# Sparse attention and expert layer on one core: late keys of diagonal tiles zeroed on GpSimd instead of pushed out on TensorE

## What is computed

```python
q, k, v = (sparsify(proj(w), 1) for w in (wq, wk, wv))    # 16 heads of 16; only the largest feature of each is kept
scores = einsum('bhqd,bhkd->bhqk', q, k) / 4
scores = where(key_index > query_index, -inf, scores)      # causal
keep the 64 largest scores of each query, softmax over them
out = einsum('bhqk,bhkd->bhqd', attn, v); out = out @ wo.T
x = x + ga * out                                           # then norm, router, experts
```

## Time and profile before

| | us |
|---|---|
| runs: median (lowest to highest) | 1067.7 (1066.64 to 1073.47) |
| span of the profiled execution, first to last instruction | 1065.8 |
| TensorE, busy in the span | 914.5 |
| VectorE | 662.4 |
| ScalarE | 480.1 |
| GpSimd | 268.7 |

### The profile page before, as it was taken

One profiled execution on the slowest core, in us unless ns is written; L12 is line 12 of the kernel. 1 busy time (PEld: TensorE's weight loads), 2 busy tenths in 40 slices (PEclk: granted clock), 3 DMA queues, 4 the chain that ended last, 5 costly groups with the idle time before them and its releaser, 6 DMA issues. The chain is left out here.

```text
span 1065.8 us, 17246 instructions
## 1 busy us (share of the span) xinstructions
PE 914.5 (86%) x6504; PEld 497.0 (47%) x6504; DVE 662.4 (62%) x1469; ACT 480.1 (45%) x631; POOL 268.7 (25%) x403
## 2 busy tenths in 40 slices
PE   6778999898999988999998999997204999999996
PEld 5533343444444443544445445335102666666664
DVE  6758677568587676676874775735487555543441
ACT  2635767664567745466773654661000122221110
POOL 3603222411331312122230220001003433343322
PEclk9869999999999998999998998998555999999999
DMA  4000000000100002100002011101561244442211
GB/s 145 15 1 21 1 21 1 1 1 2 61 21 1 1 2 81 60 1 2 1 1 81 2 41 44 38 1 40 198 221 37 51 114 107 112 115 41 25 20 20
DMA packets 34854, 46.57 MB, mean 44 GB/s; under 512 B 2184, under 2 KB 30928, under 8 KB 34640
## 3 DMA queue, kind: packets, MB, share of 16 engines
q1 hardware_dynamic: 28624, 36.89, 10.4%
q0 software_dynamic: 6144, 8.52, 5.0%
HBM read 32.69 MB, written 12.72 MB: 43 GB/s over the span
## 5 line engine op out<-in xcount | busy, mean ns | idle before, releaser
L947 ACT ACTIVATE p_buf<-ps 128x1024 f32<-128x1024 f32 x288 | 279.4, 1023 | 181.3 <-PE ps L424 95.6
L424 PE MATMUL ps<-qx,kd 32*128 32x512 f32 (+3 forms) x1280 | 147.0, 536 | 29.8 <-DVE p_buf L1281 26.1
L457 PE MATMUL ps<-p_buf,vv 128*17 128x512 f32 (+3 forms) x1664 | 156.1, 477 | 0.0
L2108 ACT ACTIVATE h_t<-ps,b_t 128x512 f32<-128x512 f32 x64 | 44.0, 688 | 236.7 <-PE ps L2048 236.7
L1281 DVE SCALAR_TENSOR_TENSOR p_buf<-ps,p_buf 128x1024 f32<-128x1024 f32 x64 | 76.7, 1220 | 78.0 <-ACT p_buf L947 65.0
L2048 PE MATMUL ps<-tok_t,w_sb 128*128 128x512 f32 x256 | 113.5, 602 | 0.0
L2058 PE MATMUL ps<-w_sb,h_t 128*128 128x256 f32 x512 | 112.5, 380 | 0.8 <-ACT h_t L2108 0.8
L779 POOL TENSOR_SCALAR_AFFINE_SELECT p_buf<-p_buf 128x512 f32<-128x512 f32 x64 | 42.0, 669 | 272.5 <-ACT p_buf L947 269.7
L2058 PEld LDWEIGHTS ps<-w_sb,h_t 128*128 128x128 f32 x512 | 96.6, 190 | 15.3 <-ACT h_t L2108 1.6
L424 PEld LDWEIGHTS ps<-qx,kd 32*128 32x128 f32 x1280 | 55.2, 191 | 71.6 <-issue 56.2
L365 PE MATMUL ps<-w_t,h_t 128*128 128x512 f32 (+1 forms) x224 | 78.8, 496 | 0.6 <-ACT w_t L889 0.6
(11 more groups left out here) (297 smaller groups left out, 1391.8 us busy)
## 6 DMA issues: line engine op xcount, KB each, us to landing
w_sb<-in_L_ffn_w_dram SPq DMA_DIRECT2D x16, 1024.0 KB, 8.8
h_table<-xr SPq DMA_DIRECT2D x3, 1056.0 KB, 4.6
x_in<-in_L_attn_x_dram SPq DMA_DIRECT2D x6, 512.0 KB, 3.9
out_dram<-xr SPq DMA_DIRECT2D x3, 1024.0 KB, 5.2
xr<-in_L_attn_x_dram SPq DMA_DIRECT2D x3, 1024.0 KB, 5.8
h_table<-xr SPq DMA_DIRECT2D x2, 528.0 KB, 3.0
xr<-in_L_attn_x_dram SPq DMA_DIRECT2D x2, 512.0 KB, 5.3
p_buf<-in_L_wmod_dram SPq DMA_DIRECT2D x1, 1024.0 KB, 8.6
```

Source lines behind the costliest of these rows:

```text
L424: m = pe.matmul(o, key, qx[r, par, t0:t0 + w], start=True, stop=not early)
L457: m = pe.matmul(ps[32 * h:32 * h + HD + 1, 6, o:o + w], vv[:, (gi // NG) % 2, i, HG * (gi % NG) + h, :], p_of(gi, u)[:, h, lo:lo + w], sta ...
L947: act.activation(p_of(gi, u)[:, 2 * a:2 * a + 2, :], buf(w), ACT.Exp, scale=0.25).then_inc(free_of(w)[0], 1)
L2108: act.activation(h1_t[:, f, :], ps[:, L1_BANKS[f % 3], :], ACT.Relu, bias=b1_t[:, e * FO + f:e * FO + f + 1]).then_inc(s_h1, 1)
```

## The change

The running maximum covers the first 256 queries instead of 512 (`RUN`), with the factor 0.625 in place of 0.992; the pieces beyond have no second matmul any more, and the piece of unit 0 with tile 1 has one for its first 128 queries. The matmuls with `late` are gone. GpSimd's `tri` now serves units 0, 1 and 2 too, and all diagonal tiles: eight selects a group instead of four, and `pv` of units 0, 1, 2, 3 and 8 waits for it. The calls `tri(gi, 0)` and `tri(gi, 1)` stand in GpSimd's loop directly ahead of `tri(gi, 2)`. VectorE's scan and product with the queries shrink to 256 columns, and its reduction over the other keys grows from 512 to 768. Left out below: the declaration of `late` and its select at the start, which go.

```diff
--- before.py
+++ after.py
@@ -137,8 +137,9 @@
         q_st = sf("q_st", [P, 2, NT, HG, 2, HD])
         o_tok = sf("o_tok", [P, NT, NH, HD])
 
-        mx = sf("mx", [P, 512])
-        qm = sf("qm", [P, 2, 512], BF16)
+        RUN = 256
+        mx = sf("mx", [P, RUN])
+        qm = sf("qm", [P, 2, RUN], BF16)
         k_far = sf("k_far", [P, T], BF16)
         k_max = sf("k_max", [P, 1])
         k_max1 = sf("k_max1", [P, 1])
@@ -227,7 +227,7 @@
 
         ring_at, m_at, pv_at = {}, {}, {}
 
-        DIAG = (2, 3, 8)
+        DIAG = (0, 1, 2, 3, 8)
 
         def tri_of(gi, u):
             return len(DIAG) * gi + DIAG.index(u) + 1
@@ -412,27 +412,19 @@
                         begin(("S", gi, u, a))
                     lo = 0
                     for i, t0, w in UNITS[u]:
-
-
-                        early = t0 < 512
-                        diag = early and t0 == P * i
+                        run = max(min(RUN - t0, w), 0)
                         last = (i, t0, w) == UNITS[u][-1]
                         for h in range(HG):
                             r = slice(32 * h, 32 * h + 32)
                             o = buf(("S", gi, u, h // 2))[:, h % 2, lo:lo + w]
                             key = ks[r, par, :] if i == 0 else kd[r, par, P * i:P * i + P]
-                            m = pe.matmul(o, key, qx[r, par, t0:t0 + w], start=True, stop=not early)
-                            if h % 2 and last and not early:
+                            m = pe.matmul(o, key, qx[r, par, t0:t0 + w], start=True, stop=not run)
+                            if h % 2 and last and not run:
                                 m.then_inc(full_of(("S", gi, u, h // 2))[0], 1)
-                        for h in range(HG * early):
+                        for h in range(HG * (run > 0)):
                             r = slice(32 * h, 32 * h + 32)
-                            o = buf(("S", gi, u, h // 2))[:, h % 2, lo:lo + w]
-                            m = pe.matmul(o, over[r, :], qm[r, par, t0:t0 + w], start=False, stop=not diag)
-                            if h % 2 and last and not diag:
-                                m.then_inc(full_of(("S", gi, u, h // 2))[0], 1)
-                        for h in range(HG * diag):
-                            o = buf(("S", gi, u, h // 2))[:, h % 2, lo:lo + P]
-                            m = pe.matmul(o, identb[:, :], late[:, :], start=False, stop=True)
+                            o = buf(("S", gi, u, h // 2))[:, h % 2, lo:lo + run]
+                            m = pe.matmul(o, over[r, :], qm[r, par, t0:t0 + run], start=False, stop=True)
                             if h % 2 and last:
                                 m.then_inc(full_of(("S", gi, u, h // 2))[0], 1)
                         lo += w
@@ -460,13 +452,11 @@
 
                 def pv(gi, u):
                     c = 0 if u < 3 else 1
-                    if u in (3, 8):
+                    if u in DIAG:
                         pe.wait_ge(f_tri, tri_of(gi, u))
-                    for a in range(2):
-                        if u in FIRST:
-                            pe.wait_ge(*free_of(("Z", gi, c, a)))
-                        elif u not in (3, 8):
-                            pe.wait_ge(*free_of(("S", gi, u, a)))
+                    else:
+                        for a in range(2):
+                            pe.wait_ge(*free_of(("Z", gi, c, a) if u in FIRST else ("S", gi, u, a)))
                     if gi == 0 and u == 0:
                         pe.wait_ge(f_n0, 1)
                     if u in (0, 3) and 2 * gi + c:
@@ -493,7 +483,6 @@
                         pe.drain().then_inc(f_O, 1)
 
                 def pv_late(gi):
-                    pe.wait_ge(f_tri, tri_of(gi, 2))
                     values(gi, 2, 6, 1, 256, 768, 256).then_inc(f_pv, 1)
                     pv_at[gi, 2] = len(pv_at) + 1
 
@@ -771,10 +760,10 @@
 
                 def tri(gi, u):
                     for a in range(2):
-                        pool.wait_ge(*free_of(("S", gi, u, a)))
+                        pool.wait_ge(*free_of(("Z", gi, 0, a) if u == 1 else ("S", gi, u, a)))
                     lo = 0
                     for i, t0, w in UNITS[u]:
-                        if t0 == P * i and t0 >= 512:
+                        if t0 == P * i:
                             p = p_of(gi, u)[:, :, lo:lo + P]
                             m = pool.affine_select(p, p, [[0, HG], [1, P]], ALU.is_ge, 0.0, base=0, channel_multiplier=-1)
                         lo += w
@@ -807,8 +796,7 @@
                           allow_small_or_imprecise_dtypes=True)
                 pool.iota(tile_no[:, :], [[P, NTALL]], base=0, channel_multiplier=0,
                           allow_small_or_imprecise_dtypes=True)
-                pool.memset(late[:, :], 0.0)
-                pool.memset(over[:, :], -(1.0 - 2.0 ** -7))
+                pool.memset(over[:, :], -0.625)
                 pool.memset(upto[:, :], 1.0)
                 pool.memset(tie[:, :], 0.0)
                 pool.memset(part_r[:, :], 0.0)
@@ -859,6 +846,8 @@
                         first_rstd(b + 1, 0)
                     if tiles:
                         keep(b + 1, t0)
+                    tri(gi, 0)
+                    tri(gi, 1)
                     tri(gi, 2)
                     tri(gi, 3)
                     if g == 0 or g == 3 and pre:
@@ -1118,7 +1107,7 @@
                     dve.tensor_tensor_scan(left[:, h], k_not[:, h], minus1[:, :].to_broadcast([P, 512]), TOPK + 0.5,
                                            ALU.add, ALU.add)
                     dve.drain().then_inc(f_cnr, 1)
-                    dve.tensor_tensor_scan(mx[:, :], kd[:, 0, h], kd[:, 0, h], 0.0, ALU.max, ALU.max)
+                    dve.tensor_tensor_scan(mx[:, :], kd[:, 0, 0:RUN], kd[:, 0, 0:RUN], 0.0, ALU.max, ALU.max)
                     dve.tensor_scalar(k_far[:, h], k_not[:, h], -FAR, None, ALU.mult)
                     dve.scalar_tensor_tensor(kb[:, :], k_not[:, 0:P], FAR, kd[:, 0, 0:P], ALU.mult, ALU.add)
                     dve.scalar_tensor_tensor(k_one[:, :, :], kd[:, 0, 0:P].unsqueeze(1).to_broadcast([P, HG, P]), 0.0,
@@ -1143,15 +1132,15 @@
                     dve.tensor_tensor_scan(left[:, h], k_not[:, h], minus1[:, :].to_broadcast([P, 512]), carry[:, :],
                                            ALU.add, ALU.add)
                     dve.drain()
-                    dve.tensor_reduce(k_max1[:, :], kd[:, 0, h], AX.X, ALU.max)
+                    dve.tensor_reduce(k_max1[:, :], kd[:, 0, RUN:T], AX.X, ALU.max)
                     dve.tensor_scalar(k_far[:, h], k_not[:, h], -FAR, None, ALU.mult)
                     dve.tensor_tensor(n_lo[:, :], n_lo[:, :], left[:, T - 1:T], ALU.min)
                     dve.drain()
-                    dve.tensor_tensor(k_max[:, :], mx[:, 511:512], k_max1[:, :], ALU.max)
+                    dve.tensor_tensor(k_max[:, :], mx[:, RUN - 1:RUN], k_max1[:, :], ALU.max)
                     dve.drain()
                     dve.tensor_scalar(ks[:, 0, :], ks[:, 0, :], k_max[:, :], None, ALU.subtract)
                     dve.scalar_tensor_tensor(kd[:, 0, :], kd[:, 0, :], k_max[:, :], k_far[:, :], ALU.subtract, ALU.add).then_inc(f_kp, 1)
-                    dve.scalar_tensor_tensor(qm[:, 0, :], mx[:, :], k_max[:, :], qx[:, 0, 0:512], ALU.subtract, ALU.mult)
+                    dve.scalar_tensor_tensor(qm[:, 0, :], mx[:, :], k_max[:, :], qx[:, 0, 0:RUN], ALU.subtract, ALU.mult)
 
                 def second_half_queries():
                     dve.wait_ge(f_mfree, m_at["Q1", 0] + 1)
@@ -1229,8 +1218,8 @@
                     par = n % 2
                     kx = kd[:, par, :]
 
-                    dve.tensor_tensor_scan(mx[:, :], kx[:, 0:512], kx[:, 0:512], 0.0, ALU.max, ALU.max)
-                    dve.tensor_reduce(k_max1[:, :], kx[:, 512:T], AX.X, ALU.max)
+                    dve.tensor_tensor_scan(mx[:, :], kx[:, 0:RUN], kx[:, 0:RUN], 0.0, ALU.max, ALU.max)
+                    dve.tensor_reduce(k_max1[:, :], kx[:, RUN:T], AX.X, ALU.max)
                     dve.tensor_scalar(k_far[:, :], k_not[:, :], -FAR, None, ALU.mult)
                     dve.tensor_tensor(n_lo[:, :], n_lo[:, :], left[:, T - 1:T], ALU.min)
                     dve.scalar_tensor_tensor(kb[:, :], k_not[:, 0:P], FAR, kx[:, 0:P], ALU.mult, ALU.add)
@@ -1247,7 +1236,7 @@
                 def queries(n):
                     par = n % 2
                     dve.wait_ge(f_mfree, m_at["Q1", n] + 1)
-                    dve.scalar_tensor_tensor(qm[:, par, :], mx[:, :], k_max[:, :], qx[:, par, 0:512], ALU.subtract, ALU.mult)
+                    dve.scalar_tensor_tensor(qm[:, par, :], mx[:, :], k_max[:, :], qx[:, par, 0:RUN], ALU.subtract, ALU.mult)
                     dve.scalar_tensor_tensor(uq[:, :], qx[:, par, :], 0.0, left[:, :], ALU.is_gt, ALU.mult)
                     dve.tensor_scalar(q_has[:, :], qx[:, par, 0:P], 0.0, 1024.0, ALU.is_gt, ALU.mult)
                     dve.drain().then_inc(f_uq, 1)
```

(2 more changed lines are left out.)

## The result

The changed kernel takes 1095.35 us (median of 4 runs, 1094.17 to 1095.60); the kernel before, beside it, 1070.23. The ratio is 1.0239, with a 95% interval of 1.0205 to 1.0273: slower. The span of the profiled execution went from 1065.8 to 1092.3 us.

A forecast was written before the change was run, and what follows sets the result against it. TensorE's order of work was taken to bound the attention stage. Terms -13.5 + 16.2 + 4.6 + 2.5 - 2.3 + 12.8 = +20.3 us on the 1065.8 span gave 1086.1; adding 1.9 for the median gave 1088, range 1070 to 1104.

The forecast's parts named there:

- Tile groups: Groups 1, 2, 5, 6, 9, 10: selects queue behind keep, TensorE stalls 4.6 us, pv starts 2.7 us later; +16.2 us.
- First groups of a batch: Groups 0, 4, 8: selects queue behind first_rstd; +4.6 us for groups 4 and 8 together, +2.5 for group 0.
- Waits in all: Sign at pv's line: nine waits for GpSimd's select, six about 4.6 us, two about 4.3, one about 8, some 44 us.
- The clock: TensorE after the new stalls: eight new drops to a lower clock at 1.6 us each, +12.8 us.
- Rival (2): TensorE's clock: the stalls come but drops only change their place, giving 1075 us; chance 0.16.
- rival (3): Stalls draw longer clock drops, or VectorE slows the selects in most groups, giving 1104 us; chance 0.10.
- Groups without a stall, and VectorE: Groups 3, 7, 11 to 15 gain 1.93 us each, -13.5; less VectorE work where TensorE waits for its chain, -2.3.
- so the gain stays: In the seven groups without a stall, selects finish while TensorE is still busy, keeping the full 1.93 us per group.
- Rival (1): GpSimd hides all the selects, so only the removed work counts, giving 1034 us; chance 0.06.

The follow-up runs named there:

- order_tiles: Changed kernel with tri(gi, 0) and tri(gi, 1) called ahead of keep but still behind first_rstd on GpSimd; 1054.03 us, ratio 0.9853.
- order_all: Changed kernel with tri(gi, 0) and tri(gi, 1) called ahead of both first_rstd and keep on GpSimd; 1042.05 us, ratio 0.9738.
- fill: Changed kernel with 64 throwaway matmuls of 128 columns ahead of the select wait of unit 0's pv in the nine stalling groups; 1079.97 us, ratio 1.0090.
- max_only: Kernel before the change with only the running maximum cut to 256 queries, late-key matmuls kept; 1058.83 us, ratio 0.9898.
- no_norm: order_all with the eight VectorE instructions of second_norm(b - 1, 0) replaced by four that only signal; 1036.22 us, ratio 0.9680.
- order_norm: order_all plus tri(gi, 2) ahead of first_rstd in groups 0, 4, 8, 12, and VectorE's normalize behind unit 4's two masks; 1026.58 us, ratio 0.9603.

## Why the prediction was right

The direction, the place and nearly the size came out: +20.3 us were worked out on the span, +26.5 came.

- **Tile groups.** Predicted was a stall of 4.6 us with pv 2.7 us late; the six stalls are 4.63 to 4.93, and pv came 2.6 to 3.3 late. With a drop each the six groups were to be 25.8 us longer (16.2 + 6 x 1.6); they are 26.2 longer. Shown by order_tiles and order_all: with the two calls moved, the stalls are gone.
- **First groups of a batch.** Groups 4 and 8: stalls of 4.28 and 4.29 us, as forecast; 8.5 us longer where 7.8 were worked out. Group 0: pv 5.3 us late, as forecast, and 3.1 us net where 2.5 were taken. The wait of unit 5 that was to take up part of it shrank from 3.05 to 0.40.
- **Waits in all.** Some 44 us were forecast for pv's line in nine waits, and 44.0 in nine came; the longest, in group 0, is 7.0 where about 8 was forecast.
- **The clock.** Priced at eight drops of 1.6 us, 12.8; the experiment fill, in which most of them go while the stalls stay, gives 12 to 15. The size came out partly by luck. All nine stalls have a drop, which begins before pv can start and reaches 3.2 to 5.8 us beyond that. In groups 5, 6 and 10, which had no drop before, the group is 2.0 to 2.2 us longer than pv's delay, so a drop costs more there than the 1.6 that was taken. In groups 1, 2 and 9 it is only 0.3 to 1.4 longer than that, because an old drop is gone: unit 5's eight matmuls took 1.7 to 2.1 us there and now take 1.14. They take 1.14 in max_only too, which has no stall, so it is not the stalls that took that drop away. Over the six groups the two errors cancel: 8.9 us, where 9.6 were forecast. Rival (2), that drops only change place, is out, and the measured 1095 lies between the forecast, 1088, and rival (3), 1104.
- **Groups without a stall, and VectorE.** Here the term was mis-sized: -13.5 for the seven groups and -2.3 for VectorE were worked out, and -10.0 came in those groups for both together. The step that failed is "so the gain stays": in groups 7, 11 and 13 VectorE's chain (masks, second norm, counts, mask) is on the path to unit 5's scores, whose wait grew from 1.62 to 2.64 us in group 7, so TensorE's 1.9 us were there worth 0.4 to 0.8, in all 3.8 us less than was worked out. no_norm shows that chain, and a lower clock behind the longer wait. The other four groups are 8.0 us shorter where 7.7 were worked out for TensorE alone, so 2.0 of VectorE's 2.3 did not show. VectorE's work itself shrank less than the 0.7 us per group that were taken: scan and product fell by 0.53 and 0.27 us and the reduction grew by 0.27 (from 0.66 to 0.93), 0.53 together. These 5.8 us are nearly all of the gap of 6.2 between forecast and result.
- **Rival (1), all hidden**, is what order_all is: 1042, where 1034 was worked out for it. The change was two lines away from it.

## What to carry to other kernels

When work is moved to an engine with time to spare, ask not only how busy it is but what stands ahead of the new work in its queue, and what that waits for: here two calls that wait for VectorE, and through it for TensorE itself, stood ahead of selects that TensorE needed sooner, and the order alone decided between 2.6% faster and 2.4% slower. A wait of a few microseconds on a busy TensorE can be paid a second time by the lower clock behind it, here 12 to 15 us beside 44 us of waits; look at the length of the first matmuls after it and at the granted clock of that stretch. And a gain on one engine ends where the next chain takes over, which is not the same engine in every round of a loop.

## What was not expected

That matmuls whose results are thrown away make a kernel faster was forecast, but not by 15 us (1095.35 to 1079.97), nor that 1.8 us less of a wait could be worth 3.9 us to a group (group 4 in order_norm), because the drop behind it went as well. GpSimd's five selects take 2.98 us in groups 4 and 6 of the kernel after, but 4.25 us in group 0, where VectorE runs a scan over two inputs; the Trainium skill (GPSIMD Engine Reference, Specifications) gives shared SBUF interfaces as a reason, and the rows agree with it, but no run here took the scan away. The trace has nearly the whole difference in the first of the five: it takes 1.70 us and ends at 85.02, just after the scan (84.60); the other four take 0.68 us each, and in group 6 all five 0.63 to 0.64.
